# Expert weights split in halves ahead of their use and kept in DRAM, and a plan made in pieces: a cross-attention and mixture-of-experts kernel on one core

## What is computed

```python
h = layernorm(x)
k, v = split(ctx @ Wkv.T)                       # 1024 rows per batch
attn = phi(h @ Wq.T) @ (phi(k).T @ v) / (phi(h @ Wq.T) @ sum(phi(k)) + 1e-6)
x = x + (attn * sigmoid(h @ Wg.T + bg)) @ Wo.T
h = layernorm(x)
w, sel = top_k(h @ Wr, 2); w = softmax(w)
out = x + sum(w[j] * (h @ We[sel[j]] + be[sel[j]]) for j in (0, 1))
```

## Time and profile before

| | us |
|---|---|
| median of 3 runs | 618.32 (618.17 to 620.92) |
| span of the profiled execution | 623.2 |

### The profile page before, as it was taken

How to read it: one execution, slowest core, us unless ns; L and a number is a source line. 1 busy time by engine, 2 the same in 40 slices (tenths; PEclk the granted TensorE clock), 3 DMA queues, 4 the chain that set the end, 5 groups by cost and what they waited for, 6 DMA issues and landing times.

```text
span 623.2 us, 10341 instructions
## 1 busy us (share of the span) xinstructions
PE 565.5 (91%) x2944; PEld 473.5 (76%) x2945; DVE 343.8 (55%) x889; ACT 198.4 (32%) x348; POOL 152.9 (25%) x179
## 2 busy tenths in 40 slices
PE   6999999999999999999999995998679999988750
PEld 4888888888888788888888884887557788766540
DVE  4453276374347456327636449677886544437753
ACT  5555333534442533532443432234001111111100
POOL 3014201014000003200101436029993000054513
PEclk9999999999999999999999998899779999999985
DMA  9713101313100412200131203457557568679956
GB/s 293 265 35 110 60 1 52 121 67 134 36 0 0 168 34 101 101 0 0 57 121 58 101 25 128 153 167 244 192 161 250 168 197 278 212 257 286 402 206 184
DMA packets 39610, 84.50 MB, mean 136 GB/s; under 512 B 4640, under 2 KB 4640, under 8 KB 39584
## 3 DMA queue, kind: packets, MB, share of 16 engines
q1 hardware_dynamic: 23232, 42.75, 21.5%
q0 software_dynamic: 7424, 25.17, 11.9%
q10 hardware_dynamic: 8928, 16.26, 6.9%
HBM read 52.18 MB, written 31.98 MB: 135 GB/s over the span
## 4 chain that ended last, share of the span: by engine, by line
PE 81%; issue 6%; POOL 6%; DVE 3%; DMA 2%; DVEq 1%; ACT 1%; another core or an unknown queue 1%; POOLq 0%; SPq 0%; ACTq 0%
PE pj L1035 22%; PE pj L1037 21%; PE pj L1036 21%; PE tp L1027 5%; PE kvb L1089 5%; POOL R L490 3%; PE pj L1117 3%; PE tp L1097 2%; PE pj L1043 2%; POOL R L488 1%; DMA num<-y,gidx 1%; DVEq L948 1%; POOL wraw L481 1%; ACT L612 1%; DMA wraw<-in_L_xattn_Wkv_dram 1%
## 5 line engine op out<-in xcount | busy, mean ns | idle before, releaser
L1035 PE MATMUL pj<-R 128*128 128x512 f32 x448 | 185.0, 413 | 3.2 <-DVE R L741 3.2
L1037 PE MATMUL pj<-R 128*128 128x512 f32 x448 | 177.4, 396 | 0.0
L1036 PE MATMUL pj<-R 128*128 128x512 f32 x448 | 176.5, 394 | 0.0
L1035 PEld LDWEIGHTS pj<-R 128*128 128x128 f32 x448 | 85.4, 191 | 19.5 <-DVE R L741 4.4
L1037 PEld LDWEIGHTS pj<-R 128*128 128x128 f32 x448 | 85.0, 190 | 19.2
L1036 PEld LDWEIGHTS pj<-R 128*128 128x128 f32 x448 | 85.6, 191 | 15.6
L1035 PE MATMUL pj<-R,aux 128*128 x184 | 78.2, 425 | 20.9 <-issue 17.6
L1037 PE MATMUL pj<-R,aux 128*128 x184 | 73.9, 402 | 0.0
L1036 PE MATMUL pj<-R,aux 128*128 x184 | 73.7, 400 | 0.0
L651 ACT CAST aux<-tp 128x512 fp32r<-128x512 f32 x46 | 26.9, 585 | 114.2 <-PE tp L1097 84.5
L475 POOL TENSOR_TENSOR rstd<-rstd,mhalf 128x1 f32<-128x1 f32 (+1 forms) x20 | 13.2, 662 | 203.0 <-DVE rstd L759 203.0
(11 more groups left out here) (156 smaller groups left out, 743.0 us busy)
## 6 DMA issues: line engine op xcount, KB each, us to landing
khat<-xs SPq DMA_DIRECT2D x46, 256.0 KB
wraw<-in_L_ffn_We_dram POOLq DMA_DIRECT2D x16, 512.0 KB, 3.9
buf<-in_ctx_dram SPq DMA_DIRECT2D x15, 512.0 KB, 3.8
y<-kvbd ACTq DMA_DIRECT2D x23, 256.0 KB
y<-zeros ACTq DMA_DIRECT2D x23, 256.0 KB
wraw<-in_x_dram SPq DMA_DIRECT2D x4, 1024.0 KB, 7.7
x_rows<-gate SPq DMA_DIRECT2D x3, 1024.0 KB, 5.2
out_dram<-wraw ACTq DMA_DIRECT2D x12, 256.0 KB
```

The lines of the kernel that those rows point to most:

```text
L1035: nc.tensor.matmul(bank[:, :], s_hi(k), m_hi(k), start=(k == 0), stop=False)
L1036: nc.tensor.matmul(bank[:, :], s_hi(k), m_lo(k), start=False, stop=False)
L1037: last = nc.tensor.matmul(bank[:, :], s_lo(k), m_hi(k), start=False, stop=(k == KT - 1))
```

## The change

Blocks of `R` are dealt anew (`W_AT`): WK in 2 and 3, WV 4 and 5, WQ 6 and 7, WG 8 and 9, the turned x 10 and 11, WO 12 and 13. A DRAM tensor `we_halves` takes the halves of each expert, 16 KB per partition. GpSimd cuts expert 0 into `R` as before (`cut_first`), and experts 1 to 7 in the batches: `cut_to_dram(e, h)` writes both parts of half an expert to `aux` and stores them (1 MB), expert 1 ahead of the loop, 2b+2 and 2b+3 in round b. Each cut waits for the store before it. SP loads an expert's halves (2 MB, `load_halves`) when the block's tenants are done: experts 1 and 2 after the last v product, 3 after the last query chunk, 4 and 5 after the last gate product, 6 and 7 after the last output product, with tile loads 2, 3 and 4 placed among them. GpSimd passes the arrivals on to `we_ready` in order (`halves_in`). ScalarE's first use of `aux` for a tile waits for all stores. `plan(0)` is taken one piece behind each of the first three `qhat` steps of the last batch. SP's wait for `we_ready` before the x2 rows 0 to 3 goes, and the loop of tile loads starts one pair later.

```diff
...
     xs_dram = [nc.dram_tensor(f"xs{g}", [E * ROWS[g], D], F32, kind="Internal").ap() for g in range(2)]
     y_dram = [nc.dram_tensor(f"y{g}", [TILES[g] * P, D], F32, kind="Internal").ap() for g in range(2)]
+    wx_dram = nc.dram_tensor("we_halves", [E, P, 2 * KT * D], F32, kind="Internal").ap()
     x2_dram = nc.dram_tensor("x2_rows", [B * L, D], F32, kind="Internal").ap()
     out_rows = out.rearrange("b l d -> (b l) d")
...
         R = sb("R", [P, 2 * E, KT, D], F32R)
         WK, WV, WQ, WG, WO = range(5)
+        W_AT = [2, 4, 6, 8, 12]
+
         def w_hi(n):
-            return R[:, 2 + 2 * n, :, :]
+            return R[:, W_AT[n], :, :]
         def w_lo(n):
-            return R[:, 3 + 2 * n, :, :]
-
-        xT_hi, xT_lo = R[:, 12, :, :], R[:, 13, :, :]
+            return R[:, W_AT[n] + 1, :, :]
+
+        xT_hi, xT_lo = R[:, 10, :, :], R[:, 11, :, :]
         ctxT_hi = R[:, 14, 0:2, :].rearrange("p s (k c) -> p s k c", k=KT)
         ctxT_lo = R[:, 14, 2:4, :].rearrange("p s (k c) -> p s k c", k=KT)
         agT_hi = R[:, 15, 0:2, :].rearrange("p s (k c) -> p s k c", k=KT)
...
         x2r_late = [sem(f"x2r_late{i}") for i in range(4)]
         out_stored = [sem(f"out_stored{i}") for i in range(4)]
         e_loaded = [sem(f"e_loaded{i}") for i in range(2)]
+        wx_loaded = [sem(f"wx_loaded{e}") for e in range(1, E)]
+        wx_low, wx_stored = sem("wx_low"), sem("wx_stored")
         consts, zeroed = sem("consts"), sem("zeroed")
         w_high, w_low = sem("w_high"), sem("w_low")
         e_high, we_ready = sem("e_high"), sem("we_ready")
...
         MOE = {name: sem(name) for name in ("t_m", "h_m", "l_m", "m_done", "y_copied")}
+
+        FIRST_TILE = 0
         def mth(m):
             return m + 3
...
                 sp.dma_start(x2r[:, c % 8:c % 8 + n, :], x2_dram[c * P:(c + n) * P, :].rearrange("(t p) d -> p t d", p=P)).then_inc(loaded, 16)
+            def load_halves(e):
+
+                sp.dma_start(R[:, 2 * e:2 * e + 2, :, :].rearrange("p a k d -> p (a k d)").bitcast(F32), wx_dram[e, :, :]).then_inc(wx_loaded[e - 1], 16)
+
             PAIRS = (FIRST[1] - 3) // 2
+            sp.wait_ge(wx_stored, 16 * 2 * (E - 1))
+            sp.wait_ge(SEMS["v"], nth("v", B - 1, ST - 1))
+            load_halves(1)
+            load_halves(2)
+            sp.wait_ge(SEMS["q"], nth("q", B - 1, G - 1))
+            load_halves(3)
             sp.wait_ge(planned, 1)
             sp.wait_ge(zeroed, 1)
             with sp.Fori(0, E) as e:
...
             sp.wait_ge(SEMS["qhat"], nth("qhat", B - 1, G - 1))
             for e in range(E):
                 sp.dma_start(be_all[:, e, :], be[e:e + 1, :].broadcast_to((P, D))).then_inc(be_loaded, 16)
+            sp.wait_ge(SEMS["g"], nth("g", B - 1, TT - 1))
+            load_halves(4)
+            load_halves(5)
             load_tile(0, 2, 0)
+            sp.wait_ge(SEMS["wo"], nth("wo", B - 1, TT - 1))
+            load_tile(0, 3, 1)
+            load_halves(6)
+            load_tile(0, 4, 0)
+            load_halves(7)
             sp.wait_ge(x2_stored, 16 * B)
             sp.wait_ge(SEMS["x2"], nth("x2", B - 1, TT - 1))
             load_x2r(4, 4, x2r_loaded[1])
-            with sp.Fori(0, PAIRS - 4) as h:
+            with sp.Fori(1, PAIRS - 4) as h:
                 load_tile(0, 2 * h + 3, 1)
                 load_tile(0, 2 * h + 4, 0)
             sp.wait_ge(planned, 2)
...
                 load_tile(0, m, m % 2)
                 e = m - (FIRST[1] - E)
                 pad(1, e, bias[:, :])
-                if e == 4:
-                    sp.wait_ge(we_ready, 2 * E)
                 if e >= 4:
                     load_x2r(e - 4, 1, x2r_loaded[0])
             sp.wait_ge(padded[1], 16 * E)
...
                 pool.dma_start(e_raw[:, 2 * h:2 * h + 2, :],
                                we[e, h * 2 * P:(h + 1) * 2 * P, :].rearrange("(k p) f -> p k f", p=P)).then_inc(e_loaded[h], 16)
-            def cut_expert(e, h):
+            def load_expert_at(e, h):
+
+                pool.dma_start(e_raw[:, 2 * h:2 * h + 2, :],
+                               we[bass.ds(e, 1), h * 2 * P:(h + 1) * 2 * P, :].rearrange("a (k p) f -> p (a k) f", p=P)).then_inc(e_loaded[h], 16)
+
+            def cut_first(h):
                 ks = slice(2 * h, 2 * h + 2)
-                pool.wait_ge(e_loaded[h], 16 * (e + 1))
-                nc.gpsimd.tensor_copy(R[:, 2 * e, ks, :], e_raw[:, ks, :]).then_inc(e_high, 1)
+                pool.wait_ge(e_loaded[h], 16)
+                nc.gpsimd.tensor_copy(R[:, 0, ks, :], e_raw[:, ks, :]).then_inc(e_high, 1)
+                pool.wait_ge(e_high, h + 1)
+                nc.gpsimd.tensor_tensor(R[:, 1, ks, :], e_raw[:, ks, :], R[:, 0, ks, :].bitcast(F32),
+                                        ALU.subtract).then_inc(we_ready, 1)
+                pool.wait_ge(we_ready, h + 1)
+
+            def cut_to_dram(e, h):
+
+                ks = slice(2 * h, 2 * h + 2)
+                u = 2 * e - 2 + h
+                pool.wait_ge(e_loaded[h], 16 * e + 16)
+                pool.wait_ge(wx_stored, 16 * u)
+                passed()
+                nc.gpsimd.tensor_copy(aux[:, 0:2, :], e_raw[:, ks, :]).then_inc(e_high, 1)
                 pool.wait_ge(e_high, 2 * e + h + 1)
-                nc.gpsimd.tensor_tensor(R[:, 2 * e + 1, ks, :], e_raw[:, ks, :], R[:, 2 * e, ks, :].bitcast(F32),
-                                        ALU.subtract).then_inc(we_ready, 1)
-                if e + 1 < E:
-                    pool.wait_ge(we_ready, 2 * e + h + 1)
-                    load_expert(e + 1, h)
+                nc.gpsimd.tensor_tensor(aux[:, 2:4, :], e_raw[:, ks, :], aux[:, 0:2, :].bitcast(F32),
+                                        ALU.subtract).then_inc(wx_low, 1)
+                pool.wait_ge(wx_low, u + 1)
+                passed()
+                pool.dma_start(wx_dram[bass.ds(e, 1), :, :].rearrange("x p (a k d) -> p (x a) k d", a=2, k=KT)[:, :, ks, :],
+                               aux[:, :, :].rearrange("p (a k) d -> p a k d", a=2).bitcast(F32)).then_inc(wx_stored, 16)
             scale(0, 0, TT, "_x", 0, 0)
             pool.wait_ge(w_low, 5 * KT)
             load_expert(0, 0)
             load_expert(0, 1)
-            cut_expert(0, 0)
-            cut_expert(0, 1)
+            cut_first(0)
+            load_expert(1, 0)
+            cut_first(1)
+            load_expert(1, 1)
+            cut_to_dram(1, 0)
+            cut_to_dram(1, 1)
             start, per = n_step[0], TT + 1
             with pool.Fori(0, B - 1) as b:
                 n_step[1:] = [per, b]
+                load_expert_at(2 * b + 2, 0)
+                load_expert_at(2 * b + 2, 1)
+                cut_to_dram(2 * b + 2, 0)
+                load_expert_at(2 * b + 3, 0)
+                cut_to_dram(2 * b + 2, 1)
+                load_expert_at(2 * b + 3, 1)
                 for t in range(TT):
                     scale(1, t, 1, "_x2", b, t)
+                cut_to_dram(2 * b + 3, 0)
                 scatter(0, b, 0)
                 scatter(0, b, 1)
                 scale(0, 0, TT, "_x", b + 1, 0)
                 scatter(0, b, 2)
                 scatter(0, b, 3)
+                cut_to_dram(2 * b + 3, 1)
                 assert n_step[0] == start + per
             n_step[:] = [start + per * (B - 1), 0, 0]
             last = B - 1
-            pool.wait_ge(SEMS["v"], nth("v", last, ST - 1))
-            for h in range(4):
-                cut_expert(1 + h // 2, h % 2)
+
+            def halves_in(e):
+
+                pool.wait_ge(wx_loaded[e - 1], 16)
+                pool.sem_inc(we_ready, 2)
+
+            halves_in(1)
             for t in range(TT):
                 scale(1, t, 1, "_x2", last, t)
+            halves_in(2)
+            halves_in(3)
+            halves_in(4)
             pool.wait_ge(SEMS["wo"], nth("wo", last, TT - 1))
             nc.gpsimd.memset(bias[:, :], 0.0).then_inc(zeroed, 1)
-            for e in range(3, E):
-                for h in range(2):
-                    cut_expert(e, h)
+            halves_in(5)
+            halves_in(6)
+            halves_in(7)
             for t in range(TT):
                 scatter(1, last, t)
...
             def high_m(m, slot):
                 act.wait_ge(MOE["t_m"], mth(m))
+                if m is FIRST_TILE:
+                    act.wait_ge(wx_stored, 16 * 2 * (E - 1))
                 act.wait_ge(MOE["m_done"], mth(m - 2))
                 nc.scalar.copy(xsT_hi[:, slot, :, :], tp[slot][:, :, :]).then_inc(MOE["h_m"], 1)
...
                 link(nc.vector.bn_aggr(mv[:, 1, t, :], stats[:, :]))
                 centre(1, t, 1, "mean_x2")
-            def queries(b):
+            def queries(b, planning=()):
                 for step, kind, i in QUERIES:
                     if step == "T" and kind == "c":
                         if b is LAST:
...
                         dve.wait_ge(SEMS["expq"], nth("expq", b, i))
```

(5 more changed lines are left out.)

## The result

The changed kernel takes 617.93 us (median of 20 executions, 614.04 to 619.49), the kernel before beside it 619.85 us (20 executions, 617.49 to 622.73). The ratio of the two is 0.9957, with a 95% interval of 0.9944 to 0.997. Two more pairs gave 0.9913 (0.988 to 0.9945) and 0.9946 (0.9919 to 0.9972). So the change gains some 3 us of 620, about half a per cent, where 11.4 were forecast. The kernel before alone takes between 619.9 and 625.4 us in the four sets of runs, so each time is compared only with that of the kernel before in the same set.

A forecast was written before the change was run, and what follows sets the result against it. TensorE, 91% busy, was held by holes near 380 us and 420 to 475 us, with VectorE waiting on GpSimd's cuts in the second. Terms -9.3 + 5.1 + 10.4 - 17.6 = -11.4 us gave 606.9 us, range 597 to 618.

The forecast's parts named there:

- Part 2: Batches: moving 14 half-expert cuts into them costs +5.1 us (0 to 15).
- Part 1: Last batch, up to the first tile transpose: plan in pieces removes a 6.26 us hole and the low clock, -9.3 us.
- The transitions: Batch changes: cuts after the fourth scale make khat and TensorE 1.3 us late, three times, 3.9 us.
- the scale of batch 0: First batch: cuts delay scale from 93.94 to 98.7, and ScalarE's next cast by about 1 us.
- rival C: Batches: each of 14 cuts meets a two-input operation on the path, 14 us in place of 5.1, 616 us; chance 0.15.
- Part 3: SP's queue, tile 0 to tile 5: tile loads wait behind the experts' halves, +10.4 us.
- Part 4: Router, tile 5 to product 13: no GpSimd cuts there, 32.0 us in place of 49.6, -17.6 us.
- The tail: From product 13 on: the program moves as a block, cost nothing, 1 or 2 us either way.
- The base: Whole kernel: profiled span 623.2 lies 4.9 us above the median 618.3, a difference taken as it is.
- A: SP's queue: tile loads slip between the experts' packets, 12 us more gained, 595 us; chance 0.12.
- B: SP's queue: halves load at a lower rate, break-even 274 GB/s, 640 us at 200 GB/s; chance 0.13.
- D: Stores end later than the last v product at 367, delaying expert loads; under 2 us, kept in the forecast.

The follow-up runs named there:

- the plan alone: The kernel before with only the first plan made in pieces behind the last batch's queries: 626.44 us against 625.26, ratio 1.0016.
- the whole plan without cuts: The changed kernel with the first plan made whole ahead of the last batch's queries, as in the kernel before: 616.21 us against 620.02, ratio 0.9946.
- the first pair: The kernel before and the changed kernel, both unedited, in the first of three sets of runs: 619.85 and 617.93 us, ratio 0.9957.
- after: The changed kernel, with the whole change made to the kernel before: 617.93 us against 619.85, ratio 0.9957.
- the cuts elsewhere: The changed kernel with each cut moved behind a khat of the next batch's keys: 609.87 us, ratio 0.9843 to the kernel before.
- the cuts' arithmetic: The changed kernel with cast and subtraction of the cuts of experts 1 to 7 shrunk to 8 elements: 605.21 us against 620.02, ratio 0.9766.
- the quarters: The changed kernel with experts 4 to 7 loaded as 16 pieces of 512 KB, one behind each tile from tile 2: 606.66 us, ratio 0.98.
- a second queue: The changed kernel with the halves of experts 4 to 7 loaded from GpSimd's queue: 626.96 us against the kernel before's 625.26, ratio 1.0027.

## Why the prediction was wrong

Forecast was 606.9 us with a range of 597 to 618. The time, 617.93, is just inside the range and far from the forecast. The gain was about a quarter of the one foretold. The step that failed is Part 2, the cost of the cuts in the batches: 5.1 us in the sum, 10.2 measured.

*What bounds the kernel, and the order of the places:* right. All that moved lies where the prediction put it.

*Part 1, the hole:* the size was right (8.1 to 9.2 us for 9.3), the reason was not. "The 6.26 us go" was put down to the pieces; the plan alone kept a hole of 6.99 us and the whole plan without cuts had none. The sentence "GpSimd has no cut in this stretch any more" stands in that part and is the cause; I counted it as a help. The two edits were costed as one. That the low clock goes with the hole was right: the attention product takes 1.06 us for 2.10.

*Part 2, the batches:* the term that failed, 10.2 us (10.1 to 10.5) for 5.1. Split by batch, between the attention products of the first pair: +7.3 in the first, +2.0 and +1.1 in the next two. The transitions were priced well: 1.43 at 117.04 and 1.45 at 220.35 and 323.42, less the 0.26 they had, 3.6 us for 3.9. Two other things were mis-sized. The first is the scale of batch 0, foretold for 98.7 and its delay priced at about 1 us. These rows are GpSimd's timeline of after:

```profile
86.16 1.03 POOL L529 CAST aux<-wraw 128x1024 fp32r<-128x1024 f32 x1 [5.25 <-DMA wraw<-in_L_ffn_We_dram]
...
96.71 2.73 POOL L531 TENSOR_TENSOR aux<-wraw,aux 128x1024 fp32r<-128x1024 f32 x1
100.20 0.69 POOL L535 DMA_DIRECT2D we_halves<-aux  x1 [0.77 <-POOL aux L531]
100.82 0.79 POOL L509 DMA_DIRECT2D wraw<-in_L_ffn_We_dram  x1
101.56 0.68 POOL L498 TENSOR_TENSOR rstd<-rstd,mhalf 128x1 f32<-128x1 f32 x1
```

The cut foretold for 84 was at 86.16, since a load of the raw weights takes 6.5 us to land beside the stores (3.9 before; medians of the pages' rows of DMA issues), and two issues of 0.7 to 0.8 us stood between the last subtraction and the scale. So scale came at 101.56 and not at 98.7. Then ScalarE's timeline:

```profile
102.54 0.81 ACT L646 ACTIVATE normed<-gate,shift,rstd 128x512 f32<-128x512 f32 x1 [7.00 <-POOL shift L499]
103.26 0.56 ACT L636 CAST R<-tp 128x512 fp32r<-128x512 f32 x1
```

ScalarE had stood 7.00 us for it, and the cast queued behind it is the one that TensorE needed: 3.33 us at 104.60, and after that eight matmuls at 0.43 us apart in the main, where 0.23 is the pace (the starts at 105.17 and 108.54 lie 3.4 us apart, for 1.8); the granted clock from 105 to 108.5 us is 0.53, the lower level. That is 4.9 us for the 1 us that was put on this delay. The prediction knew the chain and didn't ask how much slack each engine had in it, nor that a stall of 3 us costs half as much again in clock. The second is the query cuts of the later batches, which have no price in the sum; rival C sets them aside since "khat and qhat are 12 operations of 0.7 us in 100 us". GpSimd's and VectorE's timelines of after in the second batch:

```profile
184.00 2.39 POOL L531 TENSOR_TENSOR aux<-wraw,aux 128x1024 fp32r<-128x1024 f32 x1
```

```profile
184.83 2.11 DVE L926 SCALAR_TENSOR_TENSOR qhat<-buf,qhat 128x512 f32<-128x512 f32 x1 [2.03 <-ACT buf L702]
```

The last qhat starts inside a subtraction and takes 2.11 us for 0.69, and attention 1 waits 0.78 for it; in the next batch it is 0.57. These parts come to 3.6 + 4.9 + 1.4 = 9.9 of the 10.5 us of this pair. The run with the cuts elsewhere shows that another place costs the batches nothing. A share of time is no price for a meeting, for the program repeats most of its meetings: 1.43 to 1.46 at each batch change in all three profiles, 3.18 to 3.33 in the first batch, while the wait at attention 2 is 0.57 in two and not there in the third.

The Trainium skill ("SBUF — State Buffer", section "SBUF: two separate sides") has this as an exclusive lock held for the whole instruction of whoever starts first. The rows agree: 184.83 + 2.11 is 0.55 us behind the subtraction's end at 186.39, room for most of an operation of 0.69. The other half, by which khat could have won and the sum come out lower, gained nothing here.

*Part 3, the queue:* the size was right (10.1 to 12.0 us for 10.4), in part by luck. Tile 2 waits 8.08 to 9.50 us for the 6 foretold. Tile 5, which was to wait about as long again for the end of the queue, waits 0.18 to 1.42. What fills the gap is a term that the sum had at nothing: after the wait at tile 2 the matmuls come 0.43 us apart at a granted clock of 0.57 (432 to 437 us), and the next tile's transpose follows 7.57 us behind, where it was 4.49 before, 3.1 us more.

The times of the queue were worked out on the clock of the old trace, without the delay of Part 2: pads at 381, tile 5 at 436.2. SP's timeline of after has them later, behind the group that loads experts 1 to 3:

```profile
376.97 13.44 SPq L373 DMA_DIRECT2D R<-we_halves  x3
392.18 12.22 SPq L365 DMA_DIRECT2D xs<-zeros  x8
406.83 1.91 SPq L360 DMA_DIRECT2D khat<-xs  x2
...
415.26 3.65 SPq L360 DMA_DIRECT2D khat<-xs  x2
```

With the plan whole, ready by 383.93, they still came at 390.13. So it was not the plan that held them but the load of expert 3, which waits for the last q product, and that product is as late as the batches are. Without the cuts' arithmetic the pads are issued at 381.69 and tile 5's transpose is at 436.05. In after the pads come at 392.18 and tile 5 at 445.59, the forecast's times and some 10 us. The rate was higher than the 390 GB/s taken: 426 in the window from 382 to 387, and 429 in the window below, in which TensorE runs at the low clock behind its wait for tile 2:

```profile
432.00:437.00 5.00, 5.00 (x19) 4.04 (x18) 0.87 (x2) 1.01 (x1) 0.00 (x0) 0.57 1.03 429
```

The sum by the 358 GB/s of the Trainium skill ("DMA: Bandwidth & Descriptors", section "Specifications"), which would have been 2.4 us worse, an estimate, falls with the 426 and 429 of those windows.

*Part 4, the router:* right (17.1 to 17.3 us for 17.6). No operation of 128x8 on VectorE takes over 0.22 us from 420 to 480, where one took 2.31 before.

*The tail:* costed at nothing. It came out at -3.0, -0.9 and +2.1 us. *The base:* the prediction took the difference between 623.2 of span and a median of 618.3 as it was. An execution of the kernel before takes its span and 1.8 to 1.9 us in every run on record that gives both, so that profile stood for an execution of some 625, above all 20 timed in that set; the difference was no property of the kernel. The median of three, 618.32, was itself 1.5 us under that of 20, and these 1.5 us are in the 11.0 by which the time missed.

With the measured terms, as means of the three pairs, the sum up to tile 13 is -0.4 + 10.2 - 8.8 + 11.2 - 17.2 = -5.0 us. The ratios give -2.7, -5.4 and -3.4. So the 8.7 us by which the gain of the first pair missed its forecast are 5.1 of the batches, 1.7 of the hole's, queue's and router's terms together less 0.4 at the start, and some 2.3 that these stretches don't account for and that stay within the spread of the part behind tile 13.

*The rivals:* A (the queue lets tiles through) didn't happen; the quarters reach what it would have given up to tile 5 by their order. B (halves under 274 GB/s) fell: 426 to 429, though a load of 2 MB takes 11.1 us from issue to landing in the median, because others stand ahead of it; its sign, "the 2 MB loads take over 8 us each", can't tell the two apart. C, the batches at 14 us and 616, was nearest in time, by another mechanism: not every cut met something, the first batch alone cost 7 us. TensorE's waits ahead of attention 3 come to 9.0 us, under C's sign of 10. D (the stores end late) cost nothing that can be seen in the change, and some 5 us in the run with the cuts elsewhere.

**What stays open:** where the spread of up to 5 us between executions of one kernel in one set of runs arises. The profiles put it between tiles 35 and 40, among y stores and gathers, but none of the runs changed anything there.

## What to carry to other kernels

When work of one engine is moved to where it has time, list the operations of its neighbour that it will overlap there, one by one with their start times, since most of the overlaps repeat from run to run; placed just behind such an operation, the same work cost the batches nothing (10 us here). Ask as well who waits for the end of the moved work: its last store came so late that 5 of the 10 us were lost in the next stage. When bulk loads share a queue with small ones that are waited for, give each small load one bulk piece of about its own size (here 512 KB for 256), and keep their order: this was worth some 10 us, and a second queue made it worse. Of two edits that touch one stall, price each alone: here one of them was worth nothing.
